# Cross attention's keys and queries as half-precision pairs: maxima scaled on VectorE, the scale in the exponential

## The reference, cut to what matters

```python
xn = _layernorm(x, ln_gamma, ln_beta)
q = (xn @ w_q).reshape(B, SQ, NUM_HEADS, DIM_HEAD)
kv = context @ w_kv
k, v = jnp.split(kv, 2, axis=-1)
...
scores = jnp.einsum('bqhd,bkhd->bhqk', q * SCALE, k)
attn = jax.nn.softmax(scores, axis=-1)
out = jnp.einsum('bhqk,bkhd->bqhd', attn, v).reshape(B, SQ, INNER)
out = out @ w_out + b_out
return out * jnp.tanh(gate[0])
```

## Time and profile before

| | us |
|---|---|
| runs: median (lowest to highest, 3 runs) | 686.4 (684.04 to 688.42) |
| profiled execution, its own time | 685.65 |
| its span in the profile | 683.7 |
| PE busy | 563.8 (82%) |
| DVE busy | 475.3 (70%) |
| ACT busy | 406.3 (59%) |
| POOL busy | 258.0 (38%) |

### The profile page before, as it was taken

One profiled execution on the slowest core, in us unless ns is written; L12 is line 12 of the kernel. 1 busy time (PEld: TensorE's weight loads), 2 busy tenths in 40 slices (PEclk: granted clock), 3 DMA queues, 4 the chain that ended last, 5 costly groups with the idle time before them and its releaser, 6 DMA issues. The chain is left out here.

```text
span 683.7 us, 14731 instructions
## 1 busy us (share of the span) xinstructions
PE 563.8 (82%) x4972; PEld 388.7 (57%) x4972; DVE 475.3 (70%) x921; ACT 406.3 (59%) x979; POOL 258.0 (38%) x292
## 2 busy tenths in 40 slices
PE   5733768899899899999899899989769878899970
PEld 4623446566566666666566566655554554566650
DVE  2895457887887887887887887877668668533332
ACT  2484347587587587587587586575446548544431
POOL 3422023453453453353354353344425702333322
PEclk9875699999999999999999999999867999999995
DMA  8925110200210200200200201401326594333324
GB/s 255 267 54 176 37 54 32 72 36 33 71 36 31 73 31 31 73 31 31 73 31 31 73 31 31 137 31 43 114 91 221 184 342 129 60 55 61 50 32 115
DMA packets 55330, 57.36 MB, mean 84 GB/s; under 512 B 17286, under 2 KB 44238, under 8 KB 55054
## 3 DMA queue, kind: packets, MB, share of 16 engines
q1 hardware_dynamic: 50910, 50.89, 24.5%
q0 software_dynamic: 4384, 5.99, 5.1%
HBM read 46.74 MB, written 10.13 MB: 83 GB/s over the span
## 5 line engine op out<-in xcount | busy, mean ns | idle before, releaser
L734 POOL TENSOR_TENSOR c_rcp<-c_sum,neg_one 112x2 f32<-112x2 f32 x64 | 44.5, 696 | 189.7 <-ACT probs L876 189.7
L738 POOL TENSOR_TENSOR probs<-probs,c_rcp 112x750 f32<-112x750 f32 x64 | 91.8, 1435 | 5.0
L876 ACT ACTIVATE probs<-ps_s,c_neg 112x375 f32<-112x375 f32 x128 | 72.6, 578 | 27.4 <-DVE c_neg L1113 27.4
L769 ACT ACTIVATE kt_hi<-ps_o 128x376 fp32r<-128x376 f32 x64 | 31.8, 497 | 60.5 <-PE ps_o L159 60.5
L1787 POOL DMA_INDIRECT moe_sum<-gsh_hi,xs_in x21 | 33.7, 1603 | 85.7 <-ACT gsh_hi L1835 70.4
L1117 DVE SCALAR_TENSOR_TENSOR cpt_lo<-ps_t,cpt_hi 125x672 f16<-125x672 f32 x64 | 54.3, 848 | 12.4 <-ACT cpt_hi L883 12.4
L2064 PE MATMUL ps_h<-w_ex,xst_hi 128*128 (+1 forms) x168 | 57.9, 387 | 2.8 <-DVE xst_lo L1874 2.7
L1113 DVE TENSOR_REDUCE c_neg<-ps_s 112x2 f32<-112x750 f32 x64 | 59.4, 928 | 1.1 <-PE ps_s L159 1.1
L1482 PE MATMUL ps_t<-ident,probs 112*128 112x112 f32 x384 | 49.3, 265 | 6.4 <-DVE cpt_lo L1117 5.9
L1482 PEld LDWEIGHTS ps_t<-ident,probs 112*128 112x128 f32 x384 | 41.1, 143 | 16.6 <-issue 9.3
L157 PE MATMUL ps_o<-ctxt_hi,w_k_lo 128*128 128x376 f16 x128 | 42.5, 332 | 8.4 <-DVE oct_lo L1126 7.4
(11 more groups left out here) (337 smaller groups left out, 1728.5 us busy)
## 6 DMA issues: line engine op xcount, KB each, us to landing
chunk<-in_L_ffn_ew_dram SPq DMA_DIRECT2D x24, 512.0 KB, 3.3
spare<-in_L_ffn_ew_dram SPq DMA_DIRECT2D x18, 512.0 KB, 5.7
store<-in_L_ffn_ew_dram SPq DMA_DIRECT2D x6, 512.0 KB, 5.2
ctx_raw<-in_ctx_dram SPq DMA_DIRECT2D x8, 375.0 KB
moe_in<-chunk SPq DMA_DIRECT2D x1, 2709.0 KB, 13.9
plain_raw<-in_L_xattn_w_kv_dram SPq DMA_DIRECT2D x2, 1024.0 KB, 15.9
xs_in<-moe_in SPq DMA_DIRECT2D x15, 129.0 KB, 2.0
ctx_all<-in_ctx_dram SPq DMA_DIRECT2D x1, 1800.0 KB, 22.1
```

The source lines that it names most:

```text
L734: pool.tensor_tensor(c_rcp[:, s % 2, :], c_sum[:, s % 2, :], neg_one[:, :], ALU.pow).then_inc(sg["c_rcp_ready"], 1)
L738: pool.tensor_tensor(p, p, r, ALU.mult).then_inc(sg["p_normed"], 1)
L876: act.activation(probs[:, s % 2, h, 0:SK], ps_s[0:N, h, 0:SK], ACT.Exp, bias=c_neg[:, s % 2, h:h + 1], accum_out=c_sum[:, s % 2, h:h + 1]) ...
```

## The change

`qt` and `kt` become half pairs. They are scaled by fixed powers of two (2^-21 and 2^-13) instead of by `q_scale` and 1. `ps_s` then holds scores that lack the scale, which now keeps two factors of 2^-9 in place of 2^-26 (in `kc` and `qs`). The maxima go to a new tile `c_max`, and a second DVE instruction, which waits for the first on a semaphore, multiplies them by `q_scale` into `c_neg`. The exponentials get `q_scale` as their scale. ACT no longer waits for `q_scaling` ahead of the first queries. In the preparation the magnitude of WQ moves from ACT (a sum of absolute values, ahead of entry 6's `xt_hi`) to DVE (a maximum, after the rotations of entries 2 and 3), with the semaphores' counts to match.

```diff
+K_SHIFT = 2.0 ** -13
+Q_SHIFT = 2.0 ** -21
...
-                if b0 == 2:
-                    plain_magnitude(WQ)
...
-                if b0 == 0:
-                    dve.wait_ge(sg["plain2"], 16)
-                    dve.tensor_reduce(m_all[:, WVAL:WVAL + 1], plain_raw[2][:, :], X, ALU.max, apply_absolute_value=True)\
+                if b0 < 2:
+                    i = (WVAL, WQ)[b0]
+                    dve.wait_ge(sg[f"plain{i}"], 16)
+                    dve.tensor_reduce(m_all[:, i:i + 1], plain_raw[i][:, :], X, ALU.max, apply_absolute_value=True)\
                         .then_inc(sg["w_max"], 1)
...
-        qt = pair("qt", [P, PAIRS, N])
-        kt = pair("kt", [P, 2, SKP])
+        qt = half_pair(nc, ctx, "qt", [P, PAIRS, N])
+        kt = half_pair(nc, ctx, "kt", [P, 2, SKP])
...
-                else:
-                    act.wait_ge(sg["q_scaling"], 2)
                 act.activation(qt[0][:, 4 * i:4 * i + 4, :].rearrange("p a n -> p (a n)"), bank(f"Q{i}")[:, 0:4 * N], ACT.Copy,
-                               scale=q_scale[:, 0:1]).then_inc(sg["qt_hi"], 1)
+                               scale=Q_SHIFT).then_inc(sg["qt_hi"], 1)
...
-                hi(kt[0][:, p % 2, :], ps_k).then_inc(sg["kt_hi"], 1)
+                act.activation(kt[0][:, p % 2, :], ps_k, ACT.Copy, scale=K_SHIFT).then_inc(sg["kt_hi"], 1)
...
                     act.activation(probs[:, s % 2, h, 0:SK], ps_s[0:N, h, 0:SK], ACT.Exp, bias=c_neg[:, s % 2, h:h + 1],
+                                   scale=q_scale[0:N, 0:1],
                                    accum_out=c_sum[:, s % 2, h:h + 1]).then_inc(sg["c_exp"], 1)
...
-                lo(kt[1][:, p % 2, :], ps_k, kt[0][:, p % 2, :]).then_inc(sg["kt_lo"], 1)
+                dve.scalar_tensor_tensor(kt[1][:, p % 2, :], ps_k, K_SHIFT, kt[0][:, p % 2, :], op0=ALU.mult, op1=ALU.subtract)\
+                    .then_inc(sg["kt_lo"], 1)
...
-                dve.tensor_reduce(c_neg[:, s % 2, :], ps_s[0:N, :, 0:SK], X, ALU.max, negate=True).then_inc(sg["c_neg_ready"], 1)
+                dve.tensor_reduce(c_max[:, s % 2, :], ps_s[0:N, :, 0:SK], X, ALU.max, negate=True).then_inc(sg["c_max_ready"], 1)
+                dve.wait_ge(sg["c_max_ready"], PAIRS * b + s + 1)
+                dve.tensor_scalar(c_neg[:, s % 2, :], c_max[:, s % 2, :], q_scale[0:N, 0:1], None, ALU.mult)\
+                    .then_inc(sg["c_neg_ready"], 1)
```

More of the change, by code:

```diff
@@ L309, in plain_hi @@
                 act.wait_ge(sg["w_scaled"], 1)
-                act.wait_ge(sg["w_sum"], 3)
+                act.wait_ge(sg["w_sum"], 2)
                 act.activation(w[:, :, :].rearrange("p k n -> p (k n)"), plain_raw[i][:, :], ACT.Copy,
@@ L405, in weight_scales @@
                     .then_inc(sg["w_pow"], 1)
-                dve.scalar_tensor_tensor(consts["qs"][:, :], w_p[:, WQ:WQ + 1], CROSS_SCALE * 2.0 ** -26, w_p[:, XN:XN + 1],
+                dve.scalar_tensor_tensor(consts["qs"][:, :], w_p[:, WQ:WQ + 1], CROSS_SCALE * 2.0 ** -9, w_p[:, XN:XN + 1],
                                          op0=ALU.mult, op1=ALU.mult).then_inc(sg["q_consts"], 1)
@@ L504, in _ @@
                     if b0 == 2 and i == 1:
-                        pe.wait_ge(sg["w_sum"], 3)
-                        pe.wait_ge(sg["w_max"], 2)
+                        pe.wait_ge(sg["w_sum"], 2)
+                        pe.wait_ge(sg["w_max"], 3)
                         pe.transpose(ps_w[0:5, 0, 0:P], m_all[:, :], ident[:, :]).then_inc(sg["w_col_full"], 1)
@@ L590, in attention_block @@
         c_neg = sb("c_neg", [N, 2, 2])
+        c_max = sb("c_max", [N, 2, 2])
         c_sum = sb("c_sum", [N, 2, 2])
@@ L1096, in q_lo @@
                 sl = slice(4 * i, 4 * i + 4)
-                dve.scalar_tensor_tensor(qt[1][:, sl, :].rearrange("p a n -> p (a n)"), bank(f"Q{i}")[:, 0:4 * N], q_scale[:, 0:1],
-                                         qt[0][:, sl, :].rearrange("p a n -> p (a n)").bitcast(F32), op0=ALU.mult, op1=ALU.subtract)\
+                dve.scalar_tensor_tensor(qt[1][:, sl, :].rearrange("p a n -> p (a n)"), bank(f"Q{i}")[:, 0:4 * N], Q_SHIFT,
+                                         qt[0][:, sl, :].rearrange("p a n -> p (a n)"), op0=ALU.mult, op1=ALU.subtract)\
                     .then_inc(sg["qt_lo"], 1)
@@ L1181, in _ @@
             dve.tensor_scalar(v_scale[:, :], v_scale[:, :], 2.0 ** 12, None, ALU.mult).then_inc(sg["v_scaling"], 1)
-            dve.scalar_tensor_tensor(kc[:, :], v_pow[:, 0:1], 2.0 ** -26, w_p[:, WKEY:WKEY + 1], op0=ALU.mult, op1=ALU.mult)\
+            dve.scalar_tensor_tensor(kc[:, :], v_pow[:, 0:1], 2.0 ** -9, w_p[:, WKEY:WKEY + 1], op0=ALU.mult, op1=ALU.mult)\
                 .then_inc(sg["q_scaling"], 1)
```

## The result

| | before | after |
|---|---|---|
| median (lowest to highest, 6 runs each) | 686.7 (684.04 to 688.42) | 698.85 (695.65 to 701.25) |
| profiled execution, its own time (span) | 685.65 (683.7) | 697.96 (696.1) |
| PE, DVE, ACT busy | 563.8, 475.3, 406.3 | 557.8, 491.4, 412.9 |

The ratio is 1.0185, 95% interval 1.0163 to 1.0207 (11.2 to 14.2 us); between the medians lie 12.15 us. The forecast was 698 with a range of 687 to 707.

The account below looks back on a forecast made before the run. PE, ACT and DVE take turns on one chain, decided by maxima and exponentials. 1.6 us a round, 11.2 over seven, +1 for the last eight pairs and -0.1 made +12 on 686.4: 698 us, range 687 to 707.

Parts of the forecast that it names:

- Step 1: PE's 64 score blocks in half precision: 0.11 us shorter each, counted as 0 on the path.
- Step 2: Splits of keys and queries: `kt_lo` 545 ns, no change; `kt_hi` 0; `qt_hi` about 0.08 us less each, -0.1 us in all.
- Step 3: Maxima as two DVE instructions: DVE held 0.27 us more per pair and `c_neg` 0.27 later, bounds 0.14 and 0.40.
- Step 4: Per-partition scale in ACT's 128 exponentials: 0.085 us each, 0.17 per pair, bounds 0 and 0.1.
- Step 5: Preparation, WQ's magnitude from ACT to DVE: covered by DVE's waits for PE, 0, at most 0.2 us.
- s = 3, 4 and 5: Pairs where DVE's delay reaches PE's transposes: +0.27 us each per round.
- s = 6 with s = 7: At s = 6 the delay of `c_neg` and both exponentials count, +0.44 us; at s = 7 PE is late, 0.
- s = 0: First pair of an entry: `c_neg` and exponentials hold up `v_self`, `oct_lo` and PE, 0.44 less some slack, +0.3 us.
- s = 1 and 2: At s = 1 ACT has a small pause, +0.1 us taken; at s = 2 DVE waits 1.37 us for `cpt_hi`, 0.
- PE is the bound: Rival: DVE's extra time vanishes in its pauses and PE's shorter score blocks save 7 us, 679 us; chance 0.09.
- Taken up: Rival: two thirds of DVE's and ACT's additions fall into pauses, PE's gain pays part: 689 us, 684 to 692; chance 0.17.
- The clock falls more often: Rival: longer PE pauses lower the clock in most rounds, 10 us on top, 708 us; chance 0.14.

Follow-up runs that it names:

- two_step_maxima: The kernel before, with a second DVE instruction that waits for the maxima and multiplies them by one: 693.3 us, ratio 1.0114 to before.
- scaled_exponential: The kernel before, with a per-partition operand of ones as the exponentials' scale: 690.4 us, ratio 1.0062 to before.
- half_alone: The kernel after, with the query scale as an immediate, maxima and exponentials as in the kernel before: 685.9 us, ratio 1.0005 to before.
- unrelated_second: The kernel before, with a small DVE instruction behind each maxima reduction that waits for nothing and that nothing waits for: 690.3 us, ratio 1.0064 to before.
- scale_on_queries_chunks: scale_on_queries with weight-chunk maxima moved on DVE from s = 3 to 6 and s = 7 to the next entry's s = 1: 684.4 us, ratio 0.9967 to before.
- scale_on_queries: The kernel after, with the data's scale on the queries' splits again, maxima and exponentials as before: 688.1 us, ratio 1.0022 to before.

## Why the prediction was right, step by step

**The sum.** +12 forecast, +12.15 between the medians, 12.7 by the ratio. In the profile a round gave +1.70 (three against three: 52.47 against 50.77), forecast 1.6 to 1.65, and the seven of them 11.4 without the disturbed one's 1.65, forecast 11.2. The last eight pairs gave 1.10, forecast 1; their granted clock was 0.91 before and 0.94 after, so that this agrees is in part luck. The rest nearly cancels: the first scores came 1.2 later (99.77 against 98.57), the experts took 0.4 more (177.57 against 177.20), and before had one round with the clock at 0.97 worth 1.65, which this execution had not: 1.2 + 11.4 + 1.1 + 0.4 - 1.65 = 12.4, the difference of the spans. Of the 1.2 by which the first scores came later, 0.4 was there at 57 us already; the rest goes with a lower clock from 70 us on, 0.69 against 0.76 before. It isn't put down to the change: with the kernel before's preparation the first scores came between 98.11 (two_step_maxima) and 100.09 (scaled_exponential). So 12 rests on the rounds, and that the profile's other terms cancel is luck.

**Step 1, scores in half precision.** Nothing on the path: right, shown by half_alone. The size was off: 0.07 a block and not 0.11. The first step went to 0.21 and not to 0.17. So the rival with PE as the bound would have been 4.5 us and not 7.

**Step 2, the splits.** `kt_lo` 542 ns against 545 forecast, and `kt_hi` the same: right. `qt_hi` fell from 634 to 544 ns, as foreseen; its -0.1 us ahead of the loop is too small for the first scores to show.

**Step 3, the maxima.** +0.27 per pair forecast, 0.26 measured, made up of 0.13 for the instruction and 0.13 for the lost overlap. The choice of the middle between 0.14 and 0.40 held. With the 0.14 a pair and some 8 us that the prediction drew from the Trainium skill, "VectorE: DVE Perf Modes", section "The DRAIN you can't avoid", the forecast would have been 4 short; unrelated_second, which holds DVE for just that much, cost 4.2 us where two_step_maxima cost 7.8.

**Step 4, the exponentials.** 578 to 669 ns, +0.091 against 0.085 forecast. That agrees with the 93 ns in the Trainium skill, "ScalarE: Activation LUTs", section "What ACT_TABLE_LOAD costs": here it holds with two pointer operands in one instruction.

**Step 5, the preparation.** Covered: right within what can be told.

**The pairs.** s = 3, 4 and 5 came as forecast, 0.77 of 0.81 (the run of DVE through s = 3 and 4 has 18 instructions, not 19). The others were off, and their errors nearly cancelled, which is luck:
- s = 6 with s = 7: 0.44 forecast, 0.35 measured. The step "here the delay of `c_neg` and both exponentials count" added two delays that run side by side. Alone, the parts make 0.17 and 0.36 there, together 0.35.
- s = 0: 0.3 with the exponentials' share in it, 0.26 measured, all of it from the maxima; scaled_exponential shows 0 there. Right sum from a wrong path. PE's transposes start 0.06 behind the end of `cpt_lo`, which stands behind the maxima, and the scores of s = 1 follow 2.21 later; before, scaled_exponential and after have the same 0.05 to 0.06 and 2.21. `v_self`, behind which the prediction saw PE wait, starts only at 312.73, with these scores (312.77): it delays pair 1.
- s = 1 and 2: "between 0 and 0.4, I take +0.1" for s = 1 was 0.54, and s = 2 gave 0.27 back where I had 0. Both parts contribute (0.18 and 0.31, then -0.18 and -0.14).

PE of the kernel after at s = 0:

```profile
310.56 0.79 PE L1487 MATMUL ps_t<-ident,probs 112*128 112x112 f32 x6 [0.20 <-DVE cpt_lo L1122]
```

At s = 1 the prediction looked at the right engine and took too little. In the kernel after, DVE's scaling of the maxima, ACT's two exponentials, and the scores of s = 2 that wait for them (they overwrite the banks that the exponentials of s = 1 read):

```profile
315.65 0.23 DVE L1117 TENSOR_SCALAR c_neg<-c_max,q_scale 112x2 f32<-112x2 f32 x1
```

```profile
315.91 0.66 ACT L876 ACTIVATE probs<-ps_s,c_neg,q_scale 112x375 f32<-112x375 f32 x1
316.48 0.19 ACT L876 ACTIVATION_READ_ACCUMULATOR probs<-ps_s,c_neg,q_scale 112x1 f32 x1
316.57 0.65 ACT L876 ACTIVATE probs<-ps_s,c_neg,q_scale 112x375 f32<-112x375 f32 x1
```

```profile
317.37 0.37 PE L159 MATMUL ps_s<-kt_hi,qt_lo 64*112 64x376 f16 x2 [0.30 <-ACT probs L876]
```

The exponentials start 3.14 behind the scores of s = 1 (312.77), where before it was 2.75 (304.99 to 307.74): 0.39 of the 0.54. From their start to the next scores it is 1.46 instead of 1.31, 0.15 more. Here the two parts lie in series: the start is later by the maxima, and the exponentials behind it are longer. Over the whole kernel the scores wait for exponentials 3.5 us in 9 places; before it was 0.8 in one. In scaled_exponential `v_self` comes 0.19 later behind its pair's scores than before (5.55 against 5.36), so the exponentials' share of s = 0, which the prediction had there, is felt at s = 1. At s = 2 DVE's wait for `cpt_hi` is 0.76 instead of 1.37; that slack takes 0.27 of the loss up.

**The rivals.** "PE is the bound" fell with half_alone; its 0.46 to 0.63 less of PE's busy time in a round turned into wait. "Taken up" came true in a small way at s = 2 only. "The clock falls more often" did not happen in the kernel after, whose profile has no round at less than 1.00. Before had one such round; so had scaled_exponential, unrelated_second and scale_on_queries_chunks, and half_alone and scale_on_queries had two each, all at s = 2. The place is the forecast's, but of the five kernels that scale the maxima in a step of their own none had one, with one profiled execution each. What decides it I can't say.

## What to carry to other kernels

A constant factor moved from an operation that runs twice a round to operations behind every block of scores cost here what its instructions cost there, however small they are; count it at the place where the chain is tight, not by the elements it touches. On an engine that runs without pause a tiny dependent instruction took its own step and the overlap that its wait takes away, here 0.13 + 0.13 us, 64 times. And where two parts of a change delay the same instruction, compare their ways first: side by side (s = 6), only the later counts; one behind the other (s = 1), they add up. What a saving is worth depends on who is late: half precision gave nothing in this kernel and 0.23 us a round once DVE's run had been cut, and the same cut on DVE was worth 0.35 a round before and 0.93 after.

## What the runs showed of the hardware

- On DVE, a 112x2 multiplication of 0.22 to 0.23 us behind a reduction holds the engine 0.13 us if it waits for nothing and 0.26 if it waits for the reduction's result.
- On ACT, a 112x2 copy with a per-partition scale takes 0.30 us, and a dependent exponential starts 0.33 behind its start.
- The three matmuls of 64 rows and 376 columns that make a pair of scores step 0.26 and 0.17 with `fp32r` and 0.21 and 0.15 with 16-bit floats; the 0.27 ahead of the full-height matmul that follows at s = 4 is the same for both.
- An exponential whose bias already is a per-partition operand takes 0.091 us more with a second one, the scale.
